# A filter's spectrum worked out by GpSimd beside two self-attentions, in a twelve-layer decoder on Trainium2

## The reference, cut to what matters

```python
dt = jnp.exp(log_dt)                                   # 128
dtA = dt[:, None] * (A_re + 1j * A_im)                 # 128 x 64
dC = (C_re + 1j * C_im) * (jnp.exp(dtA) - 1.0) / (A_re + 1j * A_im)
powers = jnp.exp(dtA[:, :, None] * jnp.arange(L))      # L = 256
K = 2.0 * jnp.einsum('dn,dnl->dl', dC, powers).real
Kf = jnp.fft.rfft(K, n=2 * L, axis=-1)                 # the filter's spectrum
```

## Time and profile before

| | us |
|---|---|
| median of 3 runs | 4305.74 |
| range of the runs | 4303.53 to 4313.3 |
| the profiled execution's own time | 4302.7 |
| its span | 4301.0 |
| mean granted TensorE clock, share of full speed | 0.873 |
| busy: PE, DVE, ACT, POOL | 3334.1, 2990.1, 1872.6, 352.4 |

### The profile page before, as it was taken

One profiled execution on the slowest core, in us unless ns is written; L12 is line 12 of the kernel. 1 busy time (PEld: TensorE's weight loads), 2 busy tenths in 40 slices (PEclk: granted clock), 3 DMA queues, 4 the chain that ended last, 5 costly groups with the idle time before them and its releaser, 6 DMA issues. The chain is left out here.

```text
span 4301.0 us, 59641 instructions
## 1 busy us (share of the span) xinstructions
PE 3334.1 (78%) x24338; PEld 1735.1 (40%) x24338; DVE 2990.1 (70%) x4102; ACT 1872.6 (44%) x2168; POOL 352.4 (8%) x150
## 2 busy tenths in 40 slices
PE   5799999999999955877776884466654669477579
PEld 3433333333333324333334653223322347344357
DVE  4577777777777776699896446699998454546642
ACT  2365555565555532344442233344442236244233
POOL 0000000000000000000000000044441000000000
PEclk9899999999999978799997997666566789688789
DMA  2000000000000000100002001000000100010010
GB/s 83 9 15 8 8 15 8 8 13 10 8 8 15 1 12 13 22 8 8 9 1 94 30 2 47 1 0 0 0 0 0 41 11 30 9 40 1 1 41 6
DMA packets 21604, 68.51 MB, mean 16 GB/s; under 512 B 5201, under 2 KB 5713, under 8 KB 20434
## 3 DMA queue, kind: packets, MB, share of 16 engines
q1 hardware_dynamic: 21330, 64.69, 5.1%
HBM read 49.07 MB, written 0.52 MB: 12 GB/s over the span
## 5 line engine op out<-in xcount | busy, mean ns | idle before, releaser
L1071 PE MATMUL banks<-L0x_ring,L0x_context_rows 128*101 128x512 f32 x1600 | 734.7, 602 | 4.0 <-ACT L0x_ring L1119 4.0
L1130 ACT COPY L0x_ring<-banks 128x1024 f32<-128x1024 f32 (+1 forms) x416 | 387.1, 982 | 533.9 <-PE banks L1059 533.9
L1059 PE MATMUL banks<-L0x_q_thirds,L0x_context_thirds 32*128 32x512 f32 x4800 | 593.8, 606 | 10.3 <-DVE L0x_q_thirds L1236 5.3
L1161 DVE TENSOR_TENSOR L0x_ring<-L0x_ring,L0x_greatest 128x2048 f32<-128x2048 f32 (+1 forms) x208 | 469.9, 2268 | 10.9 <-ACT L0x_ring L1130 9.4
L1177 DVE TENSOR_TENSOR L0x_maxima<-L0x_maxima,L0x_ring 128x1024 f32<-128x1024 f32 (+1 forms) x288 | 322.8, 1162 | 201.1 <-ACT L0x_ring L1130 200.9
L1071 PEld LDWEIGHTS banks<-L0x_ring,L0x_context_rows 128*101 128x101 f32 x1600 | 253.9, 167 | 456.0 <-issue 448.9
L1119 ACT ACTIVATE L0x_ring<-L0x_ring 128x2048 f32<-128x2048 f32 (+1 forms) x208 | 386.4, 1858 | 16.6 <-DVE L0x_ring L1161 16.2
L1059 PEld LDWEIGHTS banks<-L0x_q_thirds,L0x_context_thirds 32*128 32x128 f32 x4800 | 237.1, 185 | 347.0 <-issue 306.7
L1611 ACT ACTIVATE L1x_probs<-banks 128x2048 f32<-128x2048 f32 (+1 forms) x112 | 196.6, 1755 | 252.6 <-PE banks L1540 210.8
L1644 DVE TENSOR_REDUCE L1x_maxima<-banks 128x3 f32<-128x1203 f32 (+1 forms) x176 | 241.3, 1372 | 54.1 <-PE banks L1509 54.1
L1667 DVE SCALAR_TENSOR_TENSOR L1x_probs<-L1x_probs,L1x_floor 128x1024 f32<-128x1024 f32 (+1 forms) x208 | 252.1, 1216 | 13.0 <-ACT L1x_probs L1611 13.0
(11 more groups left out here) (948 smaller groups left out, 5272.2 us busy)
## 6 DMA issues: line engine op xcount, KB each, us to landing
L0x_q_thirds<-L0x_q_context SPq DMA_DIRECT2D x180, 64.0 KB, 2.0
L1f_expert_weights<-in_L1f_experts SPq DMA_DIRECT2D x16, 512.0 KB, 10.0
L2f_expert_weights<-in_L2f_experts SPq DMA_DIRECT2D x8, 512.0 KB, 4.9
L3a_expert_weights<-in_L3a_experts SPq DMA_DIRECT2D x8, 512.0 KB, 5.6
L3f_expert_weights<-in_L3f_experts SPq DMA_DIRECT2D x8, 512.0 KB, 6.6
L1x_k<-L1x_k_rows SPq DMA_DIRECT2D x64, 50.0 KB
L0x_context_thirds<-in_context_thirds SPq DMA_DIRECT2D x1, 2496.0 KB, 14.3
L1x_context<-in_context SPq DMA_DIRECT2D x4, 600.4 KB, 4.7
```

The source lines that it names most:

```text
L1059: mm = pe.matmul(k.ps[:, score_bank(s) + i, :], thirds[group_rows(i), slot, t, :], q_thirds[group_rows(i), u // 2 % 2, t, :], start=t == 0 ...
L1071: mm = pe.matmul(k.ps[0:CW, bank, :], rows1[0:height(j), j, :], ring[0:height(j), s % RING, i, :], start=s == FIRST[u] and i == 0, stop=s ...
L1130: act.copy(ring[0:r, s % RING, 2 * p:2 * p + len(pair), :], k.ps[0:r, bank:bank + len(pair), :]).then_inc(copied, 1)
L1161: dve.tensor_tensor(o, o, greatest[:, u % 2, None, :].broadcast_to([P, len(js), 512]), ALU.subtract).then_inc(shifted, 1)
```

## The change

The elementwise stage of `filter_spectrum` is gone. Its arithmetic is written for GpSimd, with ScalarE for the exponentials and sines, and stands inside the two halves of the self-attention: `SpectrumAngles` in the first, `SpectrumProducts` in the second. `self_attention` takes an argument `beside` with hooks for the engines. What was one `scalar_tensor_tensor` on DVE is a `tensor_scalar` and a `tensor_tensor` on GpSimd. The multiples of the rates, 16 ACT instructions each before, are one `tensor_tensor` with two broadcast operands. DVE keeps two instructions, `copy_predicated` and `reciprocal`, after unit 7 of the second half. The context is loaded in the stage behind the second half, the tables and masks in the product stage, where ACT now also makes the mask row. The buffers are allocated one layer earlier.

```diff
--- before.py
+++ after.py
@@ self_attention
+            if beside:
+                beside.begin(signal)
+                @block.gpsimd
+                def _(pool):
+                    beside.gpsimd(pool)
...
                     act.copy(yT[:, first:first + n, g, :], k.ps[:, 4:4 + n, spare]).then_inc(copied, 1)
+                    if beside:
+                        beside.scalar(act, u)
+                if beside:
+                    beside.after(act)
...
                     if u + 1 < len(units):
                         reduce(u + 1)
+                    if beside:
+                        beside.vector(dve, u)
@@ the angles
+def turn_angle_apart(step, pool, angle, work, part, turns, radians):
+    step(pool.tensor_scalar(work, angle, 1.0 / (2 * float(np.pi)), turns, ALU.mult, ALU.add))
+    step(pool.tensor_scalar(work, work, MAGIC, MAGIC, ALU.add, ALU.subtract))
+    for c in (C1, C2, C3):
+        step(pool.tensor_scalar(part, work, c, None, ALU.mult))
+        step(pool.tensor_tensor(angle, angle, part, ALU.subtract))
+    step(pool.tensor_scalar(angle, angle, radians, 3.1415925, ALU.add, ALU.min))
+    return pool.tensor_scalar(angle, angle, -3.1415925, None, ALU.max)
@@ SpectrumAngles.gpsimd
+        exponential_apart(step, pool, w["log_dt"], dt, mag, em1, a.power)
...
+        turn_angle_apart(step, pool, s2, mag, em1, 0.0, 0.0).then_inc(self.bent, 1)
+        step(pool.tensor_copy(x1, th))
+        turn_angle_apart(step, pool, x1, mag, em1, 0.0, 0.0).then_inc(self.bent, 1)
+        step(pool.tensor_tensor(a.high_part, across(th), along(a.sixteens), ALU.mult))
+        turn_angle_apart(step, pool, a.high_part, a.decay, a.low_part, w["turns"], w["radians"]).then_inc(self.bent, 1)
+        step(pool.tensor_tensor(a.sines, across(th), along(a.ones), ALU.mult))
+        turn_angle_apart(step, pool, a.sines, a.decay, a.low_part, 0.0, 0.0).then_inc(self.bent, 1)
@@ SpectrumAngles.after
+        act.wait_ge(self.bent, 2)
+        act.activation(s2, s2, ACT.Sin).then_inc(self.sined, 1)
+        act.activation(x1, x1, ACT.Sin).then_inc(self.sined, 1)
+        act.wait_ge(self.bent, 3)
+        act.activation(a.high_part, a.high_part, ACT.Sin).then_inc(self.sined, 1)
+        act.wait_ge(self.bent, 4)
+        act.activation(a.low_part, a.sines, ACT.Abs).then_inc(self.sined, 1)
+        act.activation(a.sines, a.sines, ACT.Sin).then_inc(self.sined, 1)
+        act.wait_ge(self.sined, 5)
+        act.activation(a.low_part, a.low_part, ACT.Sin, scale=-1.0, bias=a.quarter).then_inc(self.sined, 1)
@@ SpectrumProducts
+        pool.tensor_tensor(a.decay, across(rate), along(a.ones), ALU.mult).then_inc(self.rated, 1)
...
+        pool.tensor_tensor(inv, inv, x1, ALU.add).then_inc(self.found, 1)
...
+        pool.wait_ge(self.chosen, 2)
...
+        step(pool.tensor_tensor(a.low_part, a.low_part, across(cA), ALU.mult))
+        step(pool.tensor_tensor(a.sines, a.sines, across(cB), ALU.mult))
+        step(pool.tensor_tensor(a.low_part, a.low_part, a.sines, ALU.add))
+        pool.wait_ge(self.exped, 2)
+        step(pool.tensor_tensor(a.low_part, a.low_part, a.decay, ALU.mult))
+        pool.tensor_tensor(a.decay, across(rate), along(a.sixteens), ALU.mult).then_inc(self.rated, 1)
+        pool.wait_ge(self.exped, 3)
+        step(pool.tensor_tensor(a.high_part, a.high_part, a.decay, ALU.mult))
+    def scalar(self, act, u):
+        if u == 0:
+            act.activation(a.small[13], a.small[1], ACT.Exp).then_inc(self.exped, 1)
+        elif u == 3:
+            act.wait_ge(self.rated, 1)
+            act.activation(a.decay, a.decay, ACT.Exp).then_inc(self.exped, 1)
+    def vector(self, dve, u):
+        if u == 7:
+            dve.wait_ge(self.found, 1)
+            dve.copy_predicated(em1, mag.bitcast(I32), x2).then_inc(self.chosen, 1)
+            dve.reciprocal(inv, inv).then_inc(self.chosen, 1)
+    def after(self, act):
+        act.wait_ge(self.rated, 2)
+        act.activation(self.a.decay, self.a.decay, ACT.Exp).then_inc(self.exped, 1)
@@ layer2_attention, the stage behind the halves
+            @block.sync
+            def _(sp):
+                ahead.load_context(sp)
@@ filter_spectrum: the elementwise stage is removed; in the product stage
+                sp.dma_start(tables[:].rearrange("p a b f -> p (a b f)"), k.dram["L2s_tables"]).then_inc(here, 16)
                 sp.dma_start(seen[:], k.dram["context_mask"]).then_inc(masks, 16)
+                sp.dma_start(mask[:], k.dram["text_mask"]).then_inc(masks, 16)
...
+                pe.wait_ge(here, 16)
...
+                act.wait_ge(masks, 32)
+                act.wait_ge(constants, 1)
+                act.activation(hidden[:], seen[:], ACT.Identity, scale=-MASKED, bias=masked[0:1, :])
```

More of the change, by code:

```diff
@@ L697, in _, with named @@
                 sp.wait_ge(self.here[layer], 16 * (bool(total) + bool(length)))
+        return self.named(layer)
+    def named(self, layer):
+        total, length = self.extent(layer)
         w = self.buffers[HOME[layer]]
@@ L3576, in filter_spectrum @@
+def filter_spectrum(k, a, spectrum, hidden, mask):
+    U, V = a.low_part, a.high_part
     with ExitStack() as ctx:
         tables = k.sb("L2s_tables", [P, 2, HIGH // 4, FREQ], ctx=ctx)
-        small = k.sb("L2s_small", [P, 14, P], ctx=ctx)
-        angle, work, ev, U, V = (k.sb("L2s_" + n, full, ctx=ctx) for n in ("angle", "work", "e", "U", "V"))
-        t1, t2 = (tiles[:, 2 * i:2 * i + 2].rearrange("p a t n -> p (a t n)").rearrange("p (n l) -> p n l", l=LOW) for i in range(2))
-        power = k.sb("L2s_two_to_n", [P, P], I32, ctx=ctx)
@@ L3582, in filter_spectrum @@
         kt = k.sb("L2s_filter", [P, HIGH // 4, P], ctx=ctx)
         seen = k.sb("L2x_mask_bytes", [1, B * CTX], U8, ctx=ctx)
-        quarter = k.sb("L2s_quarter_turn", [P, 2], ctx=ctx)
-        dt, a, th, em1, s2, nr, ni, wr, wi, mag, cA, cB, x1, x2 = (small[:, i, :] for i in range(14))
+        masked = k.sb("L2x_masked", [P, 1], ctx=ctx)
         with k.stage() as (block, signal):
-            here, masks, own, constants, rates, multiples = (signal() for _ in range(6))
-            bent, sined, exped, kept, absolute = (signal() for _ in range(5))
+            product, by_dve, by_act, spectral = signal(), signal(), signal(), signal()
+            here, masks, constants = signal(), signal(), signal()
@@ L3707, in filter_spectrum @@
-        with k.stage() as (block, signal):
-            product, by_dve, by_act, spectral = signal(), signal(), signal(), signal()
+                sp.dma_start(mask[:], k.dram["text_mask"]).then_inc(masks, 16)
+                sp.wait_ge(masks, 32)
+                sp.wait_ge(a.context_here, 16)
             def spread(i, r):
@@ L3910, in layer2_context @@
         hidden = k.sb("L2x_mask_row", [1, B * CTX], BF16, ctx=ctx)
[L3911 to L3912 removed]
+        filter_spectrum(k, ahead, spectrum, hidden, mask)
         normalise_columns(k, k.x, z0, k.zT)
@@ L4355, in build_program @@
                 k.weights.grow(2, k.weights.third)
+                if layer == "L2_attn":
+                    k.spectrum_ahead = SpectrumAhead(k, k.weights.third)
             BUILD[layer](k)
```

244 lines of the change are left out of this document (114 added, 130 removed).

## The result

The changed kernel takes 4315.08 us, median of 20 runs (4308.04 to 4325.44), beside 4307.01 for the kernel before (20 runs, 4302.43 to 4313.97): ratio 1.0019, interval of 95% 1.0012 to 1.0026. Timed once more in another session it was 4309.59 beside 4306.97: 1.0006, 0.9996 to 1.0015. The change gained nothing, where 4252.6 had been forecast. The profiled execution took 4308.04 us (span 4306.3), 5.3 more than that of before. It was the fastest of the 20, so a trace can account for 5.3 of the 8.1 us between the first two medians, and for no more.

A forecast was written before the change was run, and what follows sets the result against it. The kernel was taken as a row of stages, each bound by its slowest engine. Terms -64.9 + 7.2 + 2.5 + 0.6 + 1.5 = -53.1 us gave 4252.6 us, with an 8-in-10 range of 4240 to 4285.

The forecast's parts named there:

- What bounds the kernel: Whole kernel: a row of stages, each lasting as long as its slowest engine; GpSimd idle in both self-attention halves.
- term 1: Elementwise stage removed: PE's first product can start where that stage's first instruction stood, -64.9 us.
- Term 2: First half: GpSimd's list of 84.8 us delays ScalarE's last sines, so the half ends later, +7.2 us.
- the recorded sign of being wrong: GpSimd's list: the forecast is wrong if a `tensor_scalar` takes over 3 us.
- The bounds: GpSimd's `tensor_scalar` of 2048 columns: price between a copy, 1.89 us, and a two-input instruction, 4.52 us.
- Rival (b): GpSimd's list: a `tensor_scalar` with two operations costs what two inputs cost, 4294.5 us; chance 0.22 with prices between.
- Term 3: Projections behind the first half: PE's first matmuls run at half clock after idling, +2.5 us; bounds 0 and 14.
- Term 4: Second half: GpSimd's work fits, only ScalarE's large Exp behind unit 3 delays, +0.6 us; bounds 0 and 4.
- Term 5: Product stage: tables 1.2 us late and the mask row partly uncovered, +1.5 us; bounds 0 and 4.
- (a): First half: GpSimd is quicker, its list 70.9 us, total 4246 us; chance 0.17.
- (c): Both halves: GpSimd and VectorE shut each other out of SBUF, 81 us of waits, total 4327 us; chance 0.05.

The follow-up runs named there:

- The first experiment: Changed kernel with nine small and six large single multiplications of the first half written as multiply and add zero: 4282.21 us, ratio 0.9954.
- the version with the clamps back on GpSimd: Changed kernel with quick forms, tables loaded early, next layer's weights late, and two large clamps on GpSimd as one minimum-maximum each: 4246.75 us, ratio 0.9856.
- the two last versions: Changed kernel with quick forms, early tables and late next-layer weights: large clamps on VectorE 4244.53 us, on GpSimd as minimum-maximum 4246.75 us.
- The last probe: Changed kernel plus a stage behind its last layer, GpSimd rows alone, then beside five kinds of VectorE instruction: 4478.07 us in one run.

## Why the prediction was wrong

**What bounds the kernel** was right, and with it term 1: -64.9 us came as said. PE's first product stands 1.5 us behind the residual's last addition (2724.68 against 2722.85 + 0.29).

**Term 2 is the step that failed**, in the sentence "I take the copy, being nearest by its one operand". The forecast had +7.2, the half grew by 59.9 (2587.59 - 2522.65 - 5.00 of late start). The copy's price of 1.89 us was put on all 14 large one-input instructions; the recorded sign of being wrong, a `tensor_scalar` over 3 us, came true in twelve of them. Only two had the copy's price; eight are single operations (3.48 us dearer) and four are slow pairs (5.2 dearer): 48.6 us. Twelve small singles and five small pairs add 4.9, and the two products with both sources broadcast cost 3.81 where 4.52 was used, -1.4. 84.8 + 52.1 = 136.9; measured 137.5 (2444.29 to 2581.82). What had been counted, the instructions and the waits, was right to a microsecond. The first experiment took back 20.8 of it in six large rows by naming a second operation.

The bounds failed with it. I had taken a two-input instruction, 4.5 us, as the dear end; the single operation is at 5.37 and the pair at 7.1, above both ends. Rival (b) had the right term, a dear `tensor_scalar`, and its rule of 16 us for each us of the large ones holds: 48.6 / 14 = 3.47 us, 55.6 us, 4308. Its mechanism was not the one found: it made the number of operations the cause, and here multiply-add, with two, is cheap, while a single one is dear. (b) also stopped at 4294.5, and it had too small a share of the chances, since I had the nearest row as the middle and not as the cheap end. The sentence of the Trainium skill (GPSIMD Engine Reference, Engine selection) that one-input operations run at about line rate is borne out by the copy and the four quick pairs only; the traces decide against it for every other form tried, which take 2.8 or 3.7 times as long.

**Term 3** (+2.5 for the clock) measured +1.8: L330's matmuls take 15.73 us, 13.97 before, and start at a granted clock of 0.62 on average (second row, a stretch of 4.57 us that begins 0.1 us into them). Right in kind and near in size, though the gap ahead is 63.6 us and not 9. The length of the gap mattered little: in the version with the clamps back on GpSimd it is 5.8 us, and L330's matmuls take 15.67 us.

```profile
2587.90 15.73 PE L330 MATMUL banks<-z_columns,L_weights 128*128 128x512 f32 x32 [63.64 <-PEq L77]
```

```profile
2588.00:2592.57 4.57, 4.57 (x7) 1.95 (x8) 0.76 (x2) 0.60 (x1) 0.00 (x0) 0.62 0.00 0
```

**Term 4** (+0.6) measured +0.4. The second half went as worked out; here are DVE's two instructions behind unit 7 and GpSimd's wait for them, and ACT's last Exp with GpSimd's last product:

```profile
2643.23 0.29 DVE L3752 COPY_PREDICATED L2x_contexts<-L2x_contexts 128x128 f32<-128x128 int32 x1
2643.43 0.95 DVE L3753 RECIPROCAL L2x_contexts<-L2x_contexts 128x128 f32<-128x128 f32 x1
...
2644.53 0.46 POOL L3712 TENSOR_TENSOR L2x_contexts<-L2x_contexts 128x128 f32<-128x128 f32 x1 [23.69 <-DVE L2x_contexts L3753]
...
2683.74 4.54 POOL L3738 TENSOR_TENSOR L2x_rows<-L2x_rows,L2x_contexts 128x2048 f32<-128x2048 f32 x1 [7.02 <-ACT L2x_contexts L3757]
```

The wait of 24 us had been forecast, it is 23.69; and GpSimd's end at 2688.28 is DVE's (2687.87 + 0.42) to a hundredth.

**Term 5** (+1.5, bound 4) measured +4.9 and is the second step that failed. The mask row was hidden under the reduction, as worked out. The tables landed at 2733.8 (9.2 us after their issue at 2724.63), some 1.1 us after PE would have needed them without the hole, and before it needed them with the hole; so their lateness cost nothing. What cost was put at nothing in the sum: PE's hole of 2.71 us, in which it waits for its instructions behind the transfers, and 2.2 us of half clock, since the second set of products was issued at a granted clock of 0.50, which is 1.2 GHz. Before it had 0.74, part of it at 2.4 GHz, as the same stretch of the two traces shows, before and after:

```profile
2730.55:2735.60 5.05, 5.01 (x128) 4.71 (x128) 0.00 (x0) 0.00 (x0) 0.00 (x0) 0.74 0.01 3
```

```profile
2735.42:2742.70 7.28, 7.21 (x128) 6.91 (x128) 0.01 (x1) 5.56 (x1) 0.00 (x0) 0.50 0.01 2
```

In the kernel before, PE had stood for 66.8 us ahead of the stage; the granted clock was 0.73 in the first set, 1.00 between the sets, 0.99 in the first half of the second (to 2733.05) and 0.50 in the rest. After the change it had been at work since 2711.09 with short gaps, was at the upper level for the first 200 products (1.00), and fell in the hole (0.79 there, 0.50 behind it). The hole alone isn't the cause of the half clock, since with both transfers moved and no hole it was 0.61 and 0.50 in the second set, and +1.4 was left.

**The other rivals.** (a), GpSimd quicker: GpSimd is not quicker. That the two last versions, at 4244.5 and 4246.8, are near its 4246 is a coincidence: their lists are shorter than the one that was priced, and two transfers are moved. (c), the port: no unit got longer. DVE's `shift` kept its 0.42 us. The last probe shows that a copy from the banks and a reduction take no lock; the form of `shift`, one source in the banks and one in SBUF, wasn't probed by itself. By the rule of the Trainium skill (SBUF — State Buffer, Who interferes with whom), VectorE takes the lock with two inputs from SBUF or in its two-port modes, and all five kinds agree with it. It did bite once, in my own edit: the clamp on VectorE stretched a GpSimd row from 4.52 to 5.46 us.

The sum with the measured terms is -64.9 + 59.9 + 1.8 + 0.4 + 4.9 = +2.1.

## What to carry to other kernels

Price an instruction by its operations and not only by its shape and operands. Where the trace lacks the very one that the plan repeats, the nearest row may be its cheap end, so measure it alone before a list of it is moved. A chain moved to another engine hides only as long as that engine's list is shorter than the stage: the same numbers in the quick forms turned +2 into -48 us, and two transfers moved made it -61. A stage that is moved next to large transfers may stall without any semaphore, since an engine's instructions come over the same DMA engines; move the transfers, not the stage.

## What the runs showed of the hardware

- GpSimd's `tensor_scalar` on 128x2048 f32: 1.90 us for multiply-add, multiply-multiply, add-multiply and minimum-maximum; 5.37 to 5.40 for any single operation tried; 7.1 for add-add, add-subtract, subtract-multiply, multiply-subtract, add-minimum, multiply-minimum, multiply-maximum, minimum-minimum, maximum-add and maximum-minimum. The last differs from a quick one in order only. A single multiplication is cheaper with an addition of zero behind it, 1.90 for 5.37.
- A two-input instruction with both sources broadcast takes 3.81 us, with one 3.68, with none 4.50.
- GpSimd and VectorE wait for each other whole when VectorE runs `tensor_scalar`, a copy or a two-input sum in SBUF, and not when it copies from the banks or reduces. A VectorE `tensor_scalar` of 1.23 us lasts 6.26 beside a GpSimd row of 5.4, which itself becomes 6.21.

```profile
4366.16 6.21 POOL L4458 TENSOR_SCALAR probe<-probe 128x2048 f32<-128x2048 f32 x1
...
4367.19 6.26 DVE L4472 TENSOR_SCALAR probe<-probe 128x2048 f32<-128x2048 f32 x1
```

- PE stood for 2.2 to 2.7 us in the middle of 256 independent matmuls while 2.4 MB were on the queues (four traces), for 1.2 to 1.3 with 1.4 MB, and not at all without. It went on 1.4 to 1.5 us after the packet of its next instructions had landed, in all six.
